# A fused cross-attention and expert block: values matmuls in pairs over three buffers of probabilities, and an earlier place for the rows of maxima

## The reference

```python
def _L0_xattn_ref(query, key, value, ...):
    Q = split_heads(query @ Wq + bq); K = split_heads(key @ Wk + bk); V = split_heads(value @ Wv + bv)
    scores = jnp.einsum('bhqd,bhkd->bhqk', Q, K) / jnp.sqrt(jnp.float32(D))
    attn = jax.nn.softmax(scores, axis=-1)
    out = jnp.einsum('bhqk,bhkd->bhqd', attn, V)
    return merge_heads(out) @ Wo + bo

def _L0_ffn_ref(x, w_router, w1, w2, w3):
    expert_weights, expert_indices = top_k(softmax(xf @ w_router.T), 2)
    h = silu(xf @ w1[e]) * (xf @ w3[e]);  y = h @ w2[e]        # for each expert e
    return weighted sum of the two chosen y

x = x + jnp.tanh(g_xattn[0]) * _L0_xattn_ref(_layernorm(x), ctx_1024, ctx_1024, ...)
x = x + jnp.tanh(g_ffn[0]) * _L0_ffn_ref(_layernorm(x), ...)
```

## Time and profile before

| what | value |
|---|---|
| median of 3 runs | 988.64 us (984.35 to 989.5) |
| the profiled execution | 989.37 us, span 987.6 us, mean granted TensorE clock 0.973 |
| PE busy | 869.4 us, 88% |
| DVE, ACT, POOL busy | 489.4, 422.3, 475.2 us |
| attention stage | from the start to about 640 us |

### The profile page before, as it was taken

The page is one execution under the profiler, slowest core; times in us unless marked ns, Lnnn a source line. Parts: engine busy times, 40 slices in busy tenths (PEclk is TensorE's granted clock), DMA queues, the critical chain, the costliest instruction groups (busy, mean ns, idle before and its releaser), DMA issues.

```text
span 987.6 us, 20971 instructions
## 1 busy us (share of the span) xinstructions
PE 869.4 (88%) x7152; PEld 672.9 (68%) x7152; DVE 489.4 (50%) x1155; ACT 422.3 (43%) x1083; POOL 475.2 (48%) x565
## 2 busy tenths in 40 slices
PE   1689999999999999999999998823999999998996
PEld 1467788787778778787778877612666666666664
DVE  1365666776766866866766856560211121121111
ACT  1245555555555555555555555511222222222221
POOL 0553443454554554554554553361555555555553
PEclk9899999999999999999999999965999999999998
DMA  6556656677666655676655654063333333433342
GB/s 169 127 131 148 145 147 155 152 174 159 154 169 148 160 144 132 132 158 133 145 127 118 143 129 95 12 155 67 53 56 55 64 55 54 60 60 54 54 63 34
DMA packets 99246, 110.87 MB, mean 112 GB/s; under 512 B 28668, under 2 KB 80628, under 8 KB 99144
## 3 DMA queue, kind: packets, MB, share of 16 engines
q1 hardware_dynamic: 78936, 91.41, 40.3%
q0 software_dynamic: 18240, 16.83, 11.0%
q10 hardware_dynamic: 1968, 1.31, 0.5%
HBM read 34.11 MB, written 16.15 MB: 51 GB/s over the span
## 4 chain that ended last, share of the span: by engine, by line
PE 68%; DMA 16%; issue 7%; DVE 4%; POOL 3%; SPq 1%; ACTq 1%; POOLq 0%; ACT 0%; DVEq 0%
PE ps L1036 10%; PE ps L837 10%; PE ps L814 8%; PE ps L843 8%; PE ps L848 7%; DMA xg<-xn_scratch,idx 7%; PE ps L828 7%; DMA stack<-negmax_t 5%; PE ps L1071 5%; PE ps L984 3%; PE ps L1059 2%; DVE negmax L690 2%; POOL stack L303 1%; PE ps L937 1%; DMA out_dram<-y,idx 1%
## 5 line engine op out<-in xcount | busy, mean ns | idle before, releaser
L690 DVE TENSOR_REDUCE negmax<-ps 112x2 f32<-112x750 f32 x256 | 240.7, 940 | 176.7 <-PE ps L837 173.7
L464 ACT ACTIVATE probs<-ps 125x448 f32<-125x448 f32 x384 | 208.6, 543 | 247.3 <-PE ps L814 228.0
L814 PE MATMUL ps<-stack 97*125 97x224 f32 x768 | 192.1, 333 | 19.5 <-DMA stack<-negmax_t 16.8
L814 PEld LDWEIGHTS ps<-stack 97*125 97x125 f32 x768 | 129.8, 188 | 47.3 <-DMA stack<-negmax_t 23.7
L401 POOL DMA_INDIRECT out_dram<-y,idx x63 | 99.9, 1586 | 124.2 <-issue 84.3
L837 PE MATMUL ps<-stack 96*112 96x376 f32 x512 | 143.5, 361 | 13.1 <-DVE negmax L690 7.2
L794 DVE TENSOR_SCALAR y<-ps,idx 128x256 f32<-128x256 f32 x63 | 30.5, 484 | 234.4 <-PE ps L1071 234.4
L303 POOL DMA_DIRECT2D stack<-negmax_t x128 | 70.9, 558 | 94.3 <-ACT negmax_t L516 79.6
L534 ACT ACTIVATE silu<-ps 128x352 f32<-128x352 f32 x63 | 29.2, 463 | 201.8 <-PE ps L1036 201.8
L321 POOL TENSOR_SCALAR xn<-xa,mv,rstd 112x256 f32<-112x256 f32 x31 | 38.1, 1229 | 159.2 <-DVE rstd L568 158.9
L843 PE MATMUL ps<-wv_sb,ctx_t 128*125 128x256 f32 x384 | 99.8, 382 | 1.4 <-DVE bo_gated L729 0.9
(11 more groups left out here) (163 smaller groups left out, 1198.8 us busy)
## 6 DMA issues: line engine op xcount, KB each, us to landing
stack<-split SPq DMA_DIRECT2D x256, 150.0 KB
stack<-split SPq DMA_DIRECT2D x128, 94.0 KB
ctx_t<-in_ctx_dram SPq DMA_DIRECT2D x32, 375.0 KB, 4.9
stack<-split SPq DMA_DIRECT2D x128, 56.0 KB
out_dram<-xa SPq DMA_DIRECT2D x32, 112.0 KB, 4.0
xn_scratch<-xn SPq DMA_DIRECT2D x32, 112.0 KB, 4.1
w_sb<-in_L_ffn_w_dram SPq DMA_DIRECT2D x8, 352.0 KB
xa<-in_x_dram SPq DMA_DIRECT2D x6, 448.0 KB, 6.1
```

The costliest lines, as they stand in the source:

```text
L464: act.activation(probs[:, g % 2, ch, :], ps[0:KW, EXPB + k % 2, 0:4 * SQ], ACT.Exp).then_inc(s_exp, 1)
L690: dve.tensor_reduce(negmax[:, half, :, p4], ps[0:SQ, MAXB:MAXB + 2, 0:SK], axis=AX.X, op=ALU.max, negate=True).then_inc(s_max, 1)
L814: last = pe.matmul(ps[0:KW, EXPB + k % 2, QW * m:QW * m + QW], stack[:, b % NSLOT, p, KW * ch:KW * ch + KW], stack[:, b % NSLOT, p, SKP:KQ ...
```

## The change

The values of two groups are taken together: groups 0 and 1 at k = 7, groups 2 and 3 at k = 1 of the next step, and none at k = 4 and 10. `probs` has three buffers of a group each. ScalarE's copy of the second half's maxima moves from k = 3 to k = 2, between the exponential and the copy `pv_t`. On GpSimd `nm_rows(b, 1)` stands ahead of xn2 of image r. The two scatters wait for one values group less. Three small buffers of the tile map move to the memory that becomes free after the attention stage.

```diff
+    NPR = 3
-        probs = sb("probs", [KW, 2, KC, 4 * SQ])
+        probs = sb("probs", [KW, NPR, KC, 4 * SQ])
-        e_cmp, e_mul, e_mul2 = (sb(n, [1, TW, NE]) for n in ("e_cmp", "e_mul", "e_mul2"))
...
         idx = sb("idx", [P, NI, 2], i32)
+        e_cmp, e_mul, e_mul2 = (sb(n, [1, TW, NE]) for n in ("e_cmp", "e_mul", "e_mul2"))
...
@@ gpsimd, step(i)
+                if b is not None:
+                    nm_rows(b, 1)
                 if r is not None:
                     gp.wait_ge(s_rstd2, r + 1)
...
                     gp.tensor_scalar(xn2[:, r % GB, :], xrow(r), ...).then_inc(s_xn2, 1)
-                if b is not None:
-                    nm_rows(b, 1)
...
                 if u is not None:
-                    gp.wait_ge(s_pv, 4 * b + 1)
+                    gp.wait_ge(s_pv, 4 * b)
...
                 if u is not None:
-                    gp.wait_ge(s_pv, 4 * b + 3)
+                    gp.wait_ge(s_pv, 4 * b + 2)
@@ scalar, step(i)
                         if ch == 0:
-                            wait(act, s_pv, 4 * b + g - 1)
-                        act.activation(probs[:, g % 2, ch, :], ps[0:KW, EXPB + k % 2, 0:4 * SQ], ACT.Exp).then_inc(s_exp, 1)
+                            wait(act, s_pv, 4 * b + g - NPR + 1)
+                        act.activation(probs[:, (4 * b + g) % NPR, ch, :], ps[0:KW, EXPB + k % 2, 0:4 * SQ], ACT.Exp).then_inc(s_exp, 1)
...
+                    if k == 2 and b is not None:
+                        if a is not None:
+                            act.wait_ge(s_xn_ps, a + 1)
+                        negmax_out(b, 1, BB_)
                     if k == 2 and e is not None:
                         act.wait_ge(s_pv, 4 * e + 4)
                         wait(act, s_ot_ps, e)
                         act.activation(pv_t[:, :, :], ps[:, PVB, 0:4 * SQ], ACT.Copy).then_inc(s_pv_t, 1)
-                    if k == 3 and b is not None:
-                        if a is not None:
-                            act.wait_ge(s_xn_ps, a + 1)
-                        negmax_out(b, 1, BB_)
@@ tensor, values and step(i)
-                                         probs[:, g % 2, ch, SQ * j:SQ * j + SQ], start=(ch == 0), stop=(ch == KC - 1))
+                                         probs[:, (4 * b + g) % NPR, ch, SQ * j:SQ * j + SQ], start=(ch == 0), stop=(ch == KC - 1))
...
                     if k == 1 and e is not None:
+                        values(e, 2)
                         values(e, 3)
-                    if k % 3 == 1 and k > 1 and b is not None:
-                        values(b, k // 3 - 1)
+                    if k == 7 and b is not None:
+                        values(b, 0)
+                        values(b, 1)
                     if k % 3 != 2 and c is not None:
                         maxes(c, k // 3 * 2 + k % 3)
```

## The result

The changed kernel takes 994.88 us (median of 12 runs, 991.02 to 1001.23) against 987.7 us for the kernel before (12 runs, 980.71 to 989.96). The ratio is 1.0095, with a 95% interval of 1.0065 to 1.0124: slower by about 1%. Forecast was no change, 988 us. The profiled execution took 999.51 us with a span of 997.7, 10.1 us more than the span of before.

The account below looks back on a forecast made before the run. The prediction took PE's order of work to bound the attention stage. Pairs' cost, gains at k = 4 and 10 and the removed wait summed to -0.01 us a step, -0.3 us from 988.6: 988 us, range 976 to 1000.

Parts of the forecast that it names:

- the rows' wait: At exps(6), PE's weight load waits for the rows of negated maxima: 0.75 us a step, 24.1 us over 32 steps.
- ScalarE's copy 1.49 us earlier: Copy of the maxima, now behind exp(2), starts at 301.58 and ends at 301.82 instead of 303.31.
- The rows land at 301.82 + 3.41 = 305.23: Rows land 3.41 us after the copy, before PE asks at 305.98, so the wait at exps(6) goes.
- the sum: Per step: +1.14 for pairs, -0.14 at k = 4, -0.26 at k = 10, -0.75 for the wait: -0.01 us.
- the fourth rival: Rows still land late among SP's stack transfers; landing 1.0 us longer costs 19 us: 1007 us. Chance 0.11.
- A second group costs 0.57: A values group right behind another, at k = 1 and k = 7, adds 0.57 us; a lone one costs 0.78.
- The third rival: Every values group pays entry and exit in full; each pair costs 0.21 us more, 13 us: 1002 us. Chance 0.12.
- the drain: Array drains when tiling mode changes; adjacent values groups share one, seen as 0.17 us idle in the load behind them.
- The hold at k = 4: Without values there, maxes(3) waits for DVE's reduce(2): PE gains 0.26 us, not 0.78; mean gain 0.14.
- The hold at k = 11: value_proj waits for ACT's L508 behind exp(10): dropping values at k = 10 gains 0.31 us, not 0.78.
- The second rival: The k = 11 hold does not bite: 11 us faster, 977; with a weaker k = 4 hold, 972. Chance 0.24.
- The first four and last three steps are of other shapes; I count them like the rest: Steps at both ends of the attention stage were given the same -0.01 us a step, over 32 steps.

Follow-up runs that it names:

- the pause: The changed kernel, with SyncE stopping after 8 of its 16 stack transfers until the step's rows of maxima have landed: 986.35 us, ratio 1.0019 to the kernel before.
- pair_k10: The changed kernel, but values of group 0 alone at k = 4, groups 1 and 2 paired at k = 10, group 3 alone at k = 1: 966.56 us, ratio 0.9812.
- rows_only: The kernel before with only ScalarE's copy and the transfers of the rows of maxima moved earlier, no pairs: 966.08 us, ratio 0.9811.
- pairs_only: The changed kernel with ScalarE's copy and the transfers of the rows of maxima back in their old places: 1025.73 us, ratio 1.0420 to the kernel before.
- rows_only_sp_pause: The kernel before with the rows of maxima moved earlier, no pairs, and SyncE pausing after 8 of 16 stack transfers: 962.82 us, ratio 0.9762.

## Why the prediction was wrong, point by point

- **PE sets the attention stage, and the rows' wait is the large one: right.** Moving the rows alone gave 1.9%.
- **ScalarE's copy 1.49 us earlier: right.** It starts 1.15 us after the transpose, as worked out.
- **"The rows land at 301.82 + 3.41 = 305.23": the step that failed.** The 3.41 us from copy to landing was one step's value and was carried to another moment, as if it were a property of the transfer. In every second step it became 4.3 to 5.5 us. 10.9 us of the wait stayed (12 waits, up to 1.45 us), 9.5 of them by late rows, where the sum had it at 0 and called it covered "with 0.4 to spare". By the pause this is the queueing with SyncE's transfers, the fourth rival; its price, 19 us if each landing were 1.0 later, was too high because only half of the steps are hit. Its chance of 0.11 was too low, and the trace of the kernel before had a warning. At the old place alone the time from copy to load spread from 3.1 to 4.0 us over steps 0 to 28. And L303 issues the first half's rows too, of the same size and as soon after their copy: in the very step of the earlier trace rows these landed 6.1 us after their copy ended (307.92), and over all 128 transfers of L303 the time from issue to landing runs from 1.5 to 5.9 us. The latency depended on the moment already there.
- **A second group costs 0.57: right.** The pair takes 1.36 against 0.78, so 0.58. The third rival (0.78 each) is ruled out. The 0.17 us of idle load that the prediction takes for the drain is weak evidence for it: the same 0.17 stands ahead of L853 at 305.93, where no values precede.
- **The hold at k = 4: right in mechanism, near in size.** A step without values there loads maxes 0.05 after the reduction's end. The load is idle for 0.56 to 0.63 us in three steps of four, where about 0.5 was forecast, and for 0.86 in the routed one, which has a second hold of 0.54 at k = 10. Covering k = 4 again gave 1.1%, and 0.35 us in the ordinary step.
- **The hold at k = 11: right in place.** The waits are 0.3 to 0.5 us in 22 steps. Removing it gave 1.8%; steps 0 to 27 gained 11.5 us of it, as the 0.47 us in three steps of four had it, and the rest came behind them. The second rival, that it would not bite, is ruled out.
- **"The first four and last three steps are of other shapes; I count them like the rest": not so in the profiled execution.** The last four steps took 5.8 us more, with a window clock of 0.86 against 0.97. The span went from 987.6 to 997.7: -1.3 until the first exps, +4.8 in steps 0 to 27 (525.2 against 520.4 us), +5.8 in the last four, +0.8 behind them. So half of the loss is in steps 0 to 27 and the other half where PE waits for other engines and its clock falls. The granted clock is 1.00 over steps 0 to 27 in both profiles, and 0.87 against 0.97 over the last four; 18.3 us at 1.2 GHz lie in the last four of the changed kernel, 3.4 in those of before. What lowers it in those steps is open; the pairs of the last three steps alone are not it.

The sum's -0.3 us plus the 10.9 us that stayed gives +10.6, next to 10.1 us of span and 7 to 9 us by the medians and the ratio. This agreement is luck in good part. In steps 0 to 27 the waits for late rows are 8.2 us and the time grew by 4.8, so the other terms came out about 3 us better than the sum there; the last four steps' 5.8 us, which the sum had at nothing, fill the gap. By kind of step: the odd steps, without a late landing, are 0.1 to 0.2 us shorter than before (18.3 to 18.4 against 18.5), the even ones 0.6 to 0.7 longer (19.1 and 19.7 against 18.5 and 18.95).

## What to carry to other kernels

A latency read from one step belongs to that moment's traffic. Before a small transfer is moved, look at what the other queues have in flight at the new moment; the latency at the old place is no bound. Work that pays entry and exit may still cover another engine's reduction or copy: pair what covers nothing. Here maxes had 0.26 us of slack at k = 4 and 0.69 at k = 7 in the kernel before (there the reduction ends at 308.52 and the load comes at 309.26, less 0.05 for the hand-over), and that slack says where a group may leave; `pair_k10`, which took it from k = 7, had ordinary steps 0.12 us shorter but no time that could be told from `rows_only`. When two parts are bundled, time each alone: here one was worth 1.9% and the other cost 4.2% by itself.

## What the runs showed of the hardware that was not expected

- A transfer of 1.8 KB, issued by GpSimd in the same way each time, landed in the changed kernel between 2.7 and 5.4 us after the copy that it waits for (the later one of each pair). Where ten of SyncE's transfers had begun in the 6 us before the copy's end it was mostly late, where eight had it was early. Stopping SyncE after 8 of 16 transfers took the wait on it from 10.9 to 3.0 us.
- The late landings alternate with early ones from step to step through the whole stage, though both kinds of steps issue the same 16 stack transfers. In the early steps one or two of SyncE's issues, about 4 us ahead of the copy's end, took 1.2 to 2.3 us in place of 0.6.
- The mean granted clock differs between kernels of the same work: 0.955 in `pairs_only`, 0.967 in the changed kernel, 0.971 in the kernel before, 0.974 in `rows_only_sp_pause`. It does not go by the time alone: `rows_only` (966.08 us) has 0.970 and `pair_k10` (966.56 us) 0.966. Between the changed kernel and the one before, the difference is not in steps 0 to 27, where both have 1.00, but in the last four steps and behind them. Cause and effect were not separated.
